# Attention with a routed mixture of experts: the last tiles in a written-out order, the first maxima ahead of the value blocks, and six rows a partition summed in SBUF

## The chip, the core and the metric

The kernel runs on one core of one Trainium2 chip. The metric is the device time of one execution in microseconds (us). The kernel before took 504.38 us, the median of 3 runs (503.53 to 505.40). One more execution was profiled; it took 505.53 us.

## The reference

The input x is (4, 256, 32, 32): B = 4 images of C = 256 channels and 1024 tokens, N = 4096 tokens in all. Cut to what matters:

```
q, k, v = 1x1 convolutions of x              # 32, 32 and 256 channels
energy  = einsum('bci,bcj->bij', q, k)       # seen as (b, h, w, h, w)
attn    = softmax(energy, axis=-1)           # over the last w alone
x = gamma * einsum('bchk,bhwkv->bcwv', v, attn) + x
t = tokens of x                              # (4, 1024, 256)
u = layer_norm(t)
t = t + u @ W1 + (memory @ u) @ W2 + bias    # memory[i, j] = i - j for 0 < i - j < 33, else 0
u = layer_norm(t)
sel = sigmoid(u @ expert_sel.T)              # 32 experts, the two best per token
t = t + sum over the two best experts e of sel_e * (relu(u @ keys_e) @ values_e)
```

## The kernel before

All arithmetic is float32, in hand-written queues: each engine has a program of its own, and semaphores (`wait_ge`, `then_inc`) tie them together. An engine works strictly in the order that is written; a step that waits holds everything behind it.

**Start.** SyncE loads the weights and the first image. TensorE makes keys and queries of image 0, then value blocks: `vT` holds 8 blocks (`KB`) of 128 positions for each of two images, block (b, j) for image b. A block is two matmuls of 128x256 into PSUM (`v_proj`, L1128) and one evacuation on DVE (`v_evac`, L803), which scales by gamma and adds `gbv`, itself scaled once on DVE (L811) when the transfers of bv, gamma and bias have landed. Block (0, j) lies in one of four half banks, every later one in `v_p`, the upper half of bank 7. TensorE makes block 0, the scores of tile 0 (`energies`, L1159, 16 quick matmuls into `X`, banks 0 to 3), blocks 1 to 4, the scores of tile 1, blocks 5 to 7.

**The 32 steps (`NT`).** The tokens are 32 tiles of 128, 8 per image. Step s starts tile s and carries on earlier ones, each stage at a lag: at lag 0 scores, maximum (DVE, L874), subtraction (DVE, L878), exponential (ScalarE, L691), sum and reciprocal (DVE, L899, L905), scaling of the probabilities (GpSimd, L510); at lag 1 `attend` (TensorE, L1234, 16 passes of 128x256), the first sum t1 (DVE, L826), squares (ScalarE, L628); at lag 2 layer-norm factors (GpSimd, L481, L483), norm (ScalarE), `turn` (TensorE transposes, L1241); at lag 3 a copy and its rest (`turned`, `turned_low`, L831), `mix` (TensorE, L1196, six matmuls of 128x512), z_hi (ScalarE), and t1b = t1 + bias (GpSimd, L496, two buffers); at lag 4 z_lo (DVE, L818), `memory` (TensorE, L1217), `second_sum` (DVE, L837), second squares, factors and norm; at lag 5 `second_turn`, `logits` (L1224), exponential, sigmoid and the two best (DVE); at lag 6 the choice as 0/1 (`chosen`, `both_chosen`) and `positions` (TensorE), which counts the tokens chosen before; at lag 7 `place`, `entry_rows`, `rows_of_slots` (DVE), which give a row number for each of the token's two copies, and `send` (GpSimd, L487): two indirect scatters of 128 rows into the DRAM tensor `slot_rows`. In each of the first 24 steps TensorE also makes a value block of the next image (`proj_work`), once the first sum of the tile before is done, since block and sum share bank 7; its evacuation stands first in DVE's next step, ahead of the maximum. From tile 2 on the scores stand at the head of TensorE's step.

**The last tiles.** After step 31, a loop on each engine goes on with the same stages in steps 32 to 36; tiles 30 and 31 go together through mix, memory and logits. Six matmuls on zeros (`DRAIN_WARM`) keep TensorE active there.

**The plan.** When the last slots are known, DVE counts tokens per expert and works out which rows make which tile of work (L961 to L998), TensorE turns the table, DVE writes it (L1008). SyncE then loads the groups of rows, each with register arithmetic per transfer; 20 groups of four tiles, the first 12 in whole tiles, the rest in halves. Per group: transposes, hidden layer, outputs; results go by indirect DMA into the DRAM tensor `out`, 8192 rows, row t for a token's first expert and row N + t for its second.

**The final sum.** When everything is sent, GpSimd issues four accumulating transfers (L595), each adds 1024 rows of the second half of `out` to the first half in DRAM, in descriptors of 8 rows (8 KB), 128 of them a transfer. SyncE waits for all four, and the kernel ends.

```
sums_d = out.rearrange("(r c n k) e -> r c n (k e)", r=2, c=SUMS, k=SUM_ROWS)
for c in range(SUMS):
    g.dma_start(sums_d[0, c], sums_d[1, c], accum_op=ALU.add, ...).then_inc(stored, 16)
```

Of the kernel before, what the change touches and what calls it, by code (L numbers as in the profile page):

```python
# [21 lines left out]
P = 128  # L22
# [18 lines left out]
NB = 4  # L41
# [3 lines left out]
SUM_ROWS = 8  # L45
BLK = 8
# [4 lines left out]
DRAIN_WARM = 6  # L51
# [12 lines left out]
def attention_moe(nc, x_cm, x_tok, wqk4, bqk4, wvT, bv, gamma, w1, w2, bias, selT, keys, values, out):  # L64
    slots_d = nc.dram_tensor("slot_rows", [NE * CAP + P, ROW], F32, kind="Internal").ap()

    with ExitStack() as ctx:
# [54 lines left out]
        t1b = sb("t1b", [P, 2, C])  # L122
# [83 lines left out]
        vv_half = vv.rearrange("p b k r n -> p (b k r) n").rearrange("p (b k) n -> p b k n", k=GROUP)  # L206
        yb = vT[:, :, :, :].rearrange("p a (b k) n -> p (a b) k n", k=GROUP)
# [18 lines left out]
        BEFORE_E, BEFORE_MAX, BEFORE_SUM, BEFORE_E1 = 1, 1, 3, 5  # L226
# [40 lines left out]
        stored = sem("stored")  # L267

# [22 lines left out]
        def row_buffer(n):  # L291

            return xin[:, n % XB] if n % XB < NB else xin_far[:, n % XB - NB]

# [57 lines left out]
        def v_no(b, j):  # L352
            return b * KB + j

# [3 lines left out]
        def _(sp):  # L358
# [56 lines left out]
            for n in range(GROUPS):  # L415
                if n == NO_PAD_GROUPS:
                    sp.wait_ge(pads_done, 16 * (PB + PR))
                load_group(n)
            sp.wait_ge(stored, 16 * SUMS)

        @block.gpsimd
        def _(pool):
# [68 lines left out]
            def add_bias(t):  # L491
# [3 lines left out]
                after(pool, t2_done, t - 1)  # L495
                g.tensor_tensor(t1b[:, t % 2], t1[:, t % 3], biasb[:, :], ALU.add).then_inc(t1b_done, 1)  # L496
# [37 lines left out]
            for s in range(NT, NT + S_POS):  # L534
                for t in tiles(s, S_TURN):
                    first_factors(t)
                if s == NT:
                    send(s - S_SEND - 1)
                if s == NT + 1:
                    rows_complete(s - S_SEND)  # L540
                    scatter_rows(s - S_SEND, 0)
                for t in tiles(s, S_NORM2):
                    second_factors(t)
                for t in tiles(s, S_MIX):
                    add_bias(t)
                if s == NT:
                    send(s - S_SEND)
                elif s == NT + 1:
                    scatter_rows(s - S_SEND, 1)
                if s > NT:  # L550
                    send(s - S_POS)
# [41 lines left out]
            sums_d = out.rearrange("(r c n k) e -> r c n (k e)", r=2, c=SUMS, k=SUM_ROWS)  # L593
            for c in range(SUMS):
                g.dma_start(sums_d[0, c], sums_d[1, c], accum_op=ALU.add,  # L595
                            max_dma_last_dim=4 * SUM_ROWS * C).then_inc(stored, 16)
        @block.scalar
        def _(act):
# [118 lines left out]
            turned(NT - S_MIX)  # L717
            columns_written(NT - S_POS)
# [692 lines left out]
```

## Time and profile before

| | |
|---|---|
| median of 3 runs | 504.38 us |
| profiled execution, its own time | 505.53 us |
| its span | 503.80 us |
| TensorE busy | 397.0 us, 79% |
| DVE / ScalarE / GpSimd busy | 335.9 / 283.6 / 297.1 us |
| start to the first attend (23.03) | 23 us |
| steps 0 to 31 | to about 277.9 us |
| last tiles and plan | to about 319.5 us |
| expert groups | to about 474 us |
| final sum and end | to 503.8 us |

TensorE's busy share is a mean over stages with different limits; a stage is read by what ends last in it. The chain of waits follows the execution back from its last instruction, at each step to what released it. The time of a run contains the span and what lies around it, 1.73 us here.

### The profile page before, as it was taken

How to read it: one execution, taken by the hardware profiler on the slowest of the kernel's cores; microseconds unless marked ns; L12 is line 12 of the kernel's file. 1: busy time of each engine (PE TensorE's matmuls, PEld its weight loads, DVE VectorE, ACT ScalarE, POOL GpSimd, SP SyncE). 2: the span in 40 equal slices, each digit the busy share in tenths (PEclk: the TensorE clock that was granted, in tenths of full speed). 3: DMA queues.
4: the chain of work that ended last, by engine and by line, in shares of the span. 5: the costliest groups of instructions: out<-in, count | busy, mean ns of one | idle time of the engine just before them, and what ended most of it. 6: DMA issues, size and time to landing. Idle time of an engine off the chain costs nothing.

```text
span 503.8 us, 10424 instructions
## 1 busy us (share of the span) xinstructions
PE 397.0 (79%) x3007; PEld 307.7 (61%) x3007; DVE 335.9 (67%) x1022; ACT 283.6 (56%) x828; POOL 297.1 (59%) x386
## 2 busy tenths in 40 slices
PE   8879999999999999999999775759686757467000
PEld 3557778777878788787778563338464546356000
DVE  1856688987879787899999536536566678478000
ACT  1144767766767676778787455248655676354000
POOL 5333546766677777678888656343566655446700
PEclk9999999999999999999999857698989879799655
DMA  6998001411111111111111111476554443331195
GB/s 208 312 213 190 25 12 37 133 45 43 55 44 54 45 43 54 34 55 54 56 65 44 43 44 54 119 247 193 167 166 130 128 138 105 107 101 45 11 208 114
DMA packets 28441, 49.58 MB, mean 98 GB/s; under 512 B 6204, under 2 KB 21966, under 8 KB 27373
## 3 DMA queue, kind: packets, MB, share of 16 engines
q1 hardware_dynamic: 20512, 26.72, 20.0%
q0 software_dynamic: 7872, 22.19, 14.3%
q8 instruction: 25, 0.41, 0.4%
q14 instruction: 32, 0.26, 0.2%
HBM read 30.77 MB, written 25.73 MB: 112 GB/s over the span
## 4 chain that ended last, share of the span: by engine, by line
PE 48%; SPq 17%; issue 13%; DVE 11%; DMA 3%; ACT 2%; POOL 2%; POOLq 0%; DVEq 0%; ACTq 0%
PE bank L1234 21%; SPq L412 8%; PE bank L1196 7%; SPq L409 5%; PE bank L1128 5%; PE bank L1217 4%; PE bank L1224 3%; DVE vT L803 2%; SPq L276 2%; PE bank L1110 2%; DVE z_lo L818 2%; DMA biasb<-bias 2%; PE bank L1208 1%; PE X L1196 1%; SPq L277 1%
## 5 line engine op out<-in xcount | busy, mean ns | idle before, releaser
L1234 PE MATMUL bank<-vT,prob 128*128 128x256 f32 x512 | 116.0, 380 | 0.7 <-DVE vT L803 0.7
L580 POOL DMA_INDIRECT out<-vT,dest x80 | 78.5, 981 | 64.3 <-DVE vT L1062 42.7
L1234 PEld LDWEIGHTS bank<-vT,prob 128*128 128x128 f32 x512 | 94.9, 190 | 13.4 <-issue 1.1
L510 POOL TENSOR_TENSOR prob<-prob,ginv 128x1024 f32<-128x1024 f32 x32 | 61.3, 1916 | 25.9 <-DVE ginv L905 25.8
L487 POOL DMA_INDIRECT slot_rows<-rows,slot x64 | 64.8, 1013 | 16.2 <-issue 16.2
L481 POOL TENSOR_TENSOR rstd<-rstd,half_neg 128x1 f32<-128x1 f32 x64 | 36.0, 562 | 57.4 <-ACT rstd L632 56.1
L747 ACT ACTIVATE prob<-X 128x512 f32<-128x512 f32 x40 | 22.3, 593 | 50.9 <-remote 19.5
L691 ACT ACTIVATE prob<-prob 128x1024 f32<-128x1024 f32 x32 | 33.9, 1059 | 22.7 <-DVE prob L878 22.7
L1062 DVE SCALAR_TENSOR_TENSOR vT<-bank,wgt,vT 128x256 f32<-128x256 f32 x80 | 33.2, 478 | 16.0 <-remote 9.5
L874 DVE TENSOR_REDUCE gmax<-X 128x32 f32<-128x1024 f32 x32 | 39.2, 1224 | 5.9 <-PE X L1159 5.8
L899 DVE TENSOR_REDUCE gsum<-prob 128x32 f32<-128x1024 f32 x32 | 38.8, 1212 | 4.4 <-ACT prob L691 4.3
L878 DVE TENSOR_TENSOR prob<-X,gmax 128x1024 f32<-128x1024 f32 x32 | 39.2, 1225 | 1.1
L1076 DVE COPY rows<-values_s 64x256 f32 x112 | 37.5, 335 | 3.2 <-issue 2.0
L1128 PE MATMUL bank<-wv,xc_or_xin 128*128 128x256 f32 x128 | 33.0, 385 | 3.9 <-DVE t L826 2.7
L803 DVE SCALAR_TENSOR_TENSOR vT<-bank,gam,gbv 128x256 f32<-128x256 f32 x32 | 15.0, 479 | 29.0 <-PE bank L1128 28.9
L628 ACT ACTIVATE squares<-t,mv 128x256 f32<-128x256 f32 x64 | 31.9, 498 | 2.6 <-DVE t L826 2.5
L769 ACT ACTIVATE k_s<-keys_s 128x128 f32 x112 | 24.6, 301 | 10.3 <-issue 10.3
L1128 PEld LDWEIGHTS bank<-wv,xc_or_xin 128*128 128x128 f32 x128 | 23.5, 189 | 10.6 <-DVE t L826 3.9
L1331 PE MATMUL X<-ident,xc_or_xin 128*128 128x128 f32 x96 | 16.0, 321 | 17.4 <-DMA xc_or_xin<-slot_rows 15.7
L1196 PE MATMUL bank<-w_hi,uT_hi 128*128 128x512 f32 x60 | 28.0, 466 | 0.0
L1343 PE MATMUL X<-prob,k_s 128*128 128x256 f32 x96 | 24.8, 404 | 2.4 <-issue 1.6
L1331 PEld LDWEIGHTS X<-ident,xc_or_xin 128*128 128x128 f32 x96 | 12.7, 165 | 22.6 <-DMA xc_or_xin<-slot_rows 17.8
(203 smaller groups left out, 907.8 us busy)
## 6 DMA issues: line engine op xcount, KB each, us to landing
xc_or_xin<-slot_rows SPq DMA_DIRECT2D x32, 130.0 KB
xt<-x_tok SPq DMA_DIRECT2D x32, 128.0 KB, 2.1
values_s<-values SPq DMA_DIRECT2D x2, 2048.0 KB, 29.5
out<-out POOLq DMA_DIRECT2D x4, 1024.0 KB, 14.6
xc_or_xin<-x_cm SPq DMA_DIRECT2D x3, 1024.0 KB, 21.8
t<-slot_rows SPq DMA_DIRECT2D x16, 130.0 KB
t<-slot_rows SPq DMA_DIRECT2D x32, 65.0 KB
xc_or_xin<-slot_rows SPq DMA_DIRECT2D x32, 65.0 KB
```

The lines of the kernel that those rows point to most:

```text
L412: sp.dma_start(row_buffer(n)[r * HALF:(r + 1) * HALF, k, :], slots_d[bass.ds(start[2 * k + r], HALF), :]).then_inc(ld_rows[n % XB], 16)
L481: g.tensor_tensor(rstd[:, t % 2, 1:2], rstd[:, t % 2, 0:1], half_neg[:, :], ALU.pow).then_inc(rstd_done, 1)
L487: g.indirect_dma_start(out=slots_d, out_offset=bass.IndirectOffsetOnAxis(ap=slot[:, t % RB, r:r + 1], axis=0), in_=rows[:, t % RB, r, :], ...
L510: g.tensor_tensor(prob[:, t % 2], prob[:, t % 2], ginv[:, t % 2].unsqueeze(2).to_broadcast([P, WT * KB, W]), ALU.mult).then_inc(prob_done, 1)
L580: g.indirect_dma_start(out=out, out_offset=bass.IndirectOffsetOnAxis(ap=dest[:, n % (2 * NB), k:k + 1], axis=0), in_=yb[:, n % NB, k, :], ...
L874: v.tensor_reduce(gmax[:, s % 2].rearrange("p (w j) -> p w j", w=WT), E.rearrange("p w (j v) -> p w j v", v=W), AX.X, ALU.max).then_inc(ma ...
L878: v.tensor_tensor(prob[:, s % 2].rearrange("p (j w) v -> p w j v", w=WT), E.rearrange("p w (j v) -> p w j v", v=W), gmax[:, s % 2].rearran ...
L899: v.tensor_reduce(gsum[:, s % 2], prob[:, s % 2], AX.X, ALU.add).then_inc(sum_done, 1)
L1076: done = v.tensor_copy(into, values_s[side, bass.ds(expert[2 * k + r], 1), :].rearrange("p e n -> p (e n)"))
L1128: mm = m.matmul(dst, x, w, start=(i == 0), stop=(i == len(terms) - 1))
L1196: mm = m.matmul(hz_at(t), u[:, t % 2, a, :], w[:, a].rearrange("p s n -> p (s n)"), start=(i == 0), stop=(i == len(terms) - 1))
L1234: mm = m.matmul(av_p, pr[:, j, :], vT[:, b % 2, j, :], start=(j == 0), stop=(j == KB - 1))
```

## The change

It has three parts.

*First tiles.* On DVE, tile 0's maximum and subtraction come first, then the scaling of gbv and three value blocks. TensorE makes tile 1's scores after block 3 instead of 4. Block (1, 0) goes to the upper half of bank 4 (`v_at`), is made once six blocks of image 0 are evacuated, and is evacuated after tile 1's subtraction; the first attend waits for the 8 blocks of image 0 and no longer for that one. Tile 2's scores come on TensorE directly after the first attend, ahead of block (1, 1); the evacuation of (1, 1) still stands ahead of tile 2's maximum.

*Last tiles.* The loops over steps 32 to 36 are replaced on the four engines by written-out lists of the same calls. attend(31) now comes first on TensorE; tiles 30 and 31 are no longer paired; the six zero matmuls are two times three. t1b has three buffers, and the bias sums of tiles 29, 30 and 31 are made by DVE (`last_bias`). GpSimd sends tile 24 before the factors of tile 30.

*Final sum.* The four transfers cover the first 3328 of 4096 rows, so each has 104 descriptors. The last 768 rows of each half are loaded into `xc_or_xin` as 128 partitions of 6 rows, the first half by SyncE, the second by ScalarE; DVE adds them in two ops of 128x768; when the four transfers are done, SyncE and ScalarE each store half of the result.

```
-BEFORE_E, BEFORE_MAX, BEFORE_SUM, BEFORE_E1 = 1, 1, 3, 5
+BEFORE_E, BEFORE_SUM, BEFORE_E1 = 1, 3, 4
+TAIL_ROWS = 6
+IN_PLACE = N - TAIL_ROWS * P
-DRAIN_WARM = 6
+DRAIN_WARM = 3
+tail = xc_or_xin[:, 0:2 * TAIL_ROWS * C].rearrange("p (r n) -> p r n", r=2)
...
+def v_at(b, j):
+    return bank[4][:, C:2 * C] if (b, j) == (1, 0) else v_p
...
 # SyncE, at its end
+for i in range(NB):
+    sp.wait_ge(y_sent[i], sent_before(GROUPS))
+sp.dma_start(tail[:, 0], tail_rows(0)).then_inc(ld_tail[0], 16)
+sp.wait_ge(tail_added, 1)
 sp.wait_ge(stored, 16 * SUMS)
+sp.dma_start(tail_rows(0)[:, tail_half(0)], tail[:, 0, tail_half(0)]).then_inc(tail_stored, 16)
+sp.wait_ge(tail_stored, 32)
...
 # GpSimd
-    after(pool, t2_done, t - 1)
-    g.tensor_tensor(t1b[:, t % 2], t1[:, t % 3], biasb[:, :], ALU.add).then_inc(t1b_done, 1)
+    after(pool, t2_done, t - 2)
+    g.tensor_tensor(t1b[:, t % 3], t1[:, t % 3], biasb[:, :], ALU.add).then_inc(t1b_done, 1)
...
-for s in range(NT, NT + S_POS):
...
+send(NT - 8)
+first_factors(NT - 2)
+send(NT - 7)
+first_row(NT - 6)
+first_factors(NT - 1)
+second_factors(NT - 4)
+second_row(NT - 6)
+second_factors(NT - 3)
+send(NT - 5)
+second_factors(NT - 2)
+send(NT - 4)
+second_factors(NT - 1)
+send(NT - 3)
...
-    g.dma_start(sums_d[0, c], sums_d[1, c], accum_op=ALU.add,
+    g.dma_start(sums_d[0][c], sums_d[1][c], accum_op=ALU.add,
...
 # ScalarE, after the step loop
+turned(NT - 3)
+columns_written(NT - 6)
+second_copy(NT - 5)
+first_norm(NT - 2)
+first_squares(NT - 1)
+second_squares(NT - 4)
+turned(NT - 2)
+second_turned(NT - 5)
+z_high(NT - 3)
+z_high(NT - 2)
+logits_exp(NT - 5)
+first_norm(NT - 1)
...
+second_norm(NT - 2)
+second_squares(NT - 1)
+second_copy(NT - 3)
+second_turned(NT - 2)
...
 # DVE, start and step loop
-dve.wait_ge(ld_bcast, 48)
-v.tensor_scalar(gbv[:, :], gbv[:, :], gam[:, 0:1], None, ALU.mult).then_inc(gbv_done, 1)
-dve.wait_ge(gbv_done, 1)
-for j in range(BEFORE_MAX):
-    v_evac(0, j)
...
-    if work:
+    if work and s > 1:
         v_evac(work[0], work[1])
...
+    if s == 1:
+        v_evac(1, 0)
...
 # DVE, after the step loop
+z_low(NT - 4)
+turned_low(NT - 3)
+place_rows(NT - 7)
+chosen(NT - 6)
+both_chosen(NT - 6)
+last_bias(NT - 3)
+last_bias(NT - 2)
+first_sum(NT - 1)
+second_sum(NT - 4)
+last_bias(NT - 1)
+place_rows(NT - 6)
...
+for r in range(2):
+    dve.wait_ge(ld_tail[r], 16)
+for i in range(2):
+    v.tensor_tensor(tail[:, 0, tail_half(i)], tail[:, 0, tail_half(i)], tail[:, 1, tail_half(i)],
+                    ALU.add).then_inc(tail_added, 1)
...
 # TensorE
-    pe.wait_ge(v_out, min(t + 1 + TB, B * KB))
+    pe.wait_ge(v_out, min(t + 1 + TB, B * KB) if t > 0 else KB)
...
+attend(NT - 1)
+memory(NT - 4)
+second_turn(NT - 5)
+turn(NT - 2)
+positions(NT - 6)
+mix(NT - 3)
+mix(NT - 2)
+logits(NT - 5)
+memory(NT - 3)
+memory(NT - 2)
+turn(NT - 1)
+second_turn(NT - 4)
+positions(NT - 5)
+logits(NT - 4)
+mix(NT - 1)
+second_turn(NT - 3)
+positions(NT - 4)
+kept_warm(DRAIN_WARM)
+memory(NT - 1)
+logits(NT - 3)
+second_turn(NT - 2)
+positions(NT - 3)
+logits(NT - 2)
+kept_warm(DRAIN_WARM)
+second_turn(NT - 1)
+positions(NT - 2)
+logits(NT - 1)
+positions(NT - 1)
```

The order of DVE's instructions at its start, before. gmax is the maximum, prob the subtraction, gbv the scaled bias, vT a value block, gsum and ginv sum and reciprocal:

```order
L811 TENSOR_SCALAR gbv<-gbv,gam 128x256
L803 SCALAR_TENSOR_TENSOR vT<-bank,gam,gbv 128x256
L874 TENSOR_REDUCE gmax<-X 128x32
L878 TENSOR_TENSOR prob<-X,gmax 128x4x8x32
L803 SCALAR_TENSOR_TENSOR vT<-bank,gam,gbv 128x256 x2
L899 TENSOR_REDUCE gsum<-prob 128x32
L905 RECIPROCAL ginv<-gsum 128x32
L803 SCALAR_TENSOR_TENSOR vT<-bank,gam,gbv 128x256 x6
L874 TENSOR_REDUCE gmax<-X 128x32
```

And now, down to the same second maximum and past it:

```order
L918 TENSOR_REDUCE gmax<-X 128x32
L922 TENSOR_TENSOR prob<-X,gmax 128x4x8x32
L927 TENSOR_SCALAR gbv<-gbv,gam 128x256
L852 SCALAR_TENSOR_TENSOR vT<-bank,gam,gbv 128x256 x3
L948 TENSOR_REDUCE gsum<-prob 128x32
L954 RECIPROCAL ginv<-gsum 128x32
L852 SCALAR_TENSOR_TENSOR vT<-bank,gam,gbv 128x256 x5
L918 TENSOR_REDUCE gmax<-X 128x32
L922 TENSOR_TENSOR prob<-X,gmax 128x4x8x32
L852 SCALAR_TENSOR_TENSOR vT<-bank,gam,gbv 128x256
```

Both the first and the second maximum have one value block fewer ahead of them, and the first also no gbv.

TensorE behind the first attend, before, then now (L1128 and L1227 are a value block, L1159 and L1258 the scores of tile 2):

```order
L1234 MATMUL bank<-vT,prob 128x256 x8
L1128 MATMUL bank<-wv,xc_or_xin 128x256 x2
L1159 MATMUL X<-k_s,q_s 32x256 x16
L1234 MATMUL bank<-vT,prob 128x256 x8
L1119 MATMUL bank<-xc_or_xin,wqk 32x256 x8
```

```order
L1333 MATMUL bank<-vT,prob 128x256 x8
L1258 MATMUL X<-k_s,q_s 32x256 x16
L1227 MATMUL bank<-wv,xc_or_xin 128x256 x2
L1333 MATMUL bank<-vT,prob 128x256 x8
L1218 MATMUL bank<-xc_or_xin,wqk 32x256 x8
```

The scores of tile 2 and block (1, 1) have changed places.

TensorE after step 31, from turn(29) (first row) on, before; the attend of tile 31 comes behind the mix that begins in the last row:

```order
L1241 MATMUL bank<-ident,u 128x128 x2
L1208 MATMUL bank<-ident,rows 128x128 x2
L1217 MATMUL bank<-z_hi,band_r 128x256
L1217 MATMUL bank<-z_lo,band_r 128x256
L1217 MATMUL bank<-z_hi,band_r 128x256
L1217 MATMUL bank<-z_lo,band_r 128x256
L1224 MATMUL bank<-sels,u2T 128x32 x2
L1180 MATMUL X<-hotb,upper 128x32
L1181 MATMUL X<-seen,ones_b 128x32
L1196 MATMUL bank<-w_hi,uT_hi 128x512
```

And now (L1340 turn, L1333 attend, L1316 memory, L1307 second_turn, L1279 and L1280 positions, L1295 mix):

```order
L1340 MATMUL bank<-ident,u 128x128 x2
L1333 MATMUL bank<-vT,prob 128x256 x8
L1316 MATMUL bank<-z_hi,band_r 128x256
L1316 MATMUL bank<-z_lo,band_r 128x256
L1316 MATMUL bank<-z_hi,band_r 128x256
L1316 MATMUL bank<-z_lo,band_r 128x256
L1307 MATMUL bank<-ident,rows 128x128 x2
L1340 MATMUL bank<-ident,u 128x128 x2
L1279 MATMUL X<-hotb,upper 128x32
L1280 MATMUL X<-seen,ones_b 128x32
L1295 MATMUL bank<-w_hi,uT_hi 128x512
```

attend(31) stands directly behind turn(29), and turn(30) ahead of the first mix.

## Rows read from the trace of the kernel before

**Rows 1.** The page's chain of waits: share of the span by engine.
```profile
PE 48%; SPq 17%; issue 13%; DVE 11%; DMA 3%; ACT 2%; POOL 2%; POOLq 0%; DVEq 0%; ACTq 0%
```

**Rows 2.** Windows: length, busy by engine (instructions), granted clock, DMA share, GB/s.
```profile
278.10:281.20 3.10, 0.12 (x2) 0.02 (x1) 1.76 (x10) 1.81 (x10) 2.47 (x4) 1.00 0.00 0
280.00:300.00 20.00, 15.36 (x59) 12.47 (x60) 9.19 (x39) 8.20 (x30) 12.01 (x17) 0.71 0.12 41
300.00:320.00 20.00, 12.16 (x57) 6.67 (x56) 13.23 (x75) 7.38 (x28) 11.52 (x15) 0.67 0.19 67
477.50:499.00 21.50, 0.00 (x0) 0.00 (x0) 0.00 (x0) 0.00 (x0) 2.24 (x3) 0.50 0.99 195
12.00:20.00 8.00, 7.22 (x75) 5.31 (x60) 6.63 (x12) 2.39 (x3) 0.99 (x1) 1.00 1.10 399
```

**Rows 3.** Chain in order of time, first tiles: start, length (us), what.
```profile
4.32 8.58 DMA biasb<-bias
...
13.80 1.14 DVE gmax L874
...
22.88 1.14 DVE gmax L874
...
28.34 1.13 PE bank L1128 x4
...
30.31 1.23 DVE gmax L874
```

**Rows 4.** Timeline, first tiles: start, length, engine, line, operation.
```profile
11.48 0.71 PE L1159 MATMUL X<-k_s,q_s 32*32 32x256 f32 x32
...
18.84 2.09 DVE L803 SCALAR_TENSOR_TENSOR vT<-bank,gam,gbv 128x256 f32<-128x256 f32 x5
```

**Rows 5.** Timeline, end of step 31; in brackets the idle time before.
```profile
277.28 1.91 POOL L510 TENSOR_TENSOR prob<-prob,ginv 128x1024 f32<-128x1024 f32 x1 [0.21 <-DVE ginv L905]
...
277.54 0.38 PE L1241 MATMUL bank<-ident,u 128*128 128x128 f32 x2
...
281.18 0.38 PE L1217 MATMUL bank<-z_hi,band_r 128*128 128x256 f32 x1 [2.98 <-DVE z_lo L818]
...
285.20 3.62 PE L1234 MATMUL bank<-vT,prob 128*128 128x256 f32 x16
```

**Rows 6.** The page's costliest groups: busy us, mean ns; idle before, releaser.
```profile
L487 POOL DMA_INDIRECT slot_rows<-rows,slot x64 | 64.8, 1013 | 16.2 <-issue 16.2
...
L628 ACT ACTIVATE squares<-t,mv 128x256 f32<-128x256 f32 x64 | 31.9, 498 | 2.6 <-DVE t L826 2.5
```

**Rows 7.** Chain in order of time, last tiles and plan.
```profile
276.24 1.48 PE bank L1196 x6
...
293.98 2.75 PE X L1196 x6
...
302.73 0.44 DVE t L837 x2
...
309.02 0.43 DVE ex L928
...
310.65 0.19 DVE hotb L848
...
311.66 0.22 DVE slot L865
...
314.41 0.10 DVE full_i L961
...
319.19 0.29 DVE u L1008
```

**Rows 8.** Tile `out` (issues, landings), and the page's DMA issues (KB, us to landing).
```profile
L595 POOL DMA_DIRECT2D out<-out x4: 992/1347/1812, 476.2 to 477.9; - x4
...
DMA to landing us min/median/max: 7.9/14.6/21.6
...
slot_rows<-pad_rows SPq DMA_DIRECT2D x1, 130.0 KB, 2.3
```

More of the change, by code:

```diff
@@ new lines, in _ @@
+            columns_written(NT - 6)
[9 more added lines that the diff above has]
+            first_norm(NT - 1)
+            second_norm(NT - 4)
+            second_squares(NT - 3)
+            turned(NT - 1)
+            second_turned(NT - 4)
+            columns_written(NT - 5)
@@ L787, in _ @@
                     transposed(n + 2)
+            for i in range(NB):
+                act.wait_ge(y_sent[i], sent_before(GROUPS))
+            a.dma_start(tail[:, 1], tail_rows(1)).then_inc(ld_tail[1], 16)
+            act.wait_ge(tail_added, 2)
+            act.wait_ge(stored, 16 * SUMS)
+            a.dma_start(tail_rows(0)[:, tail_half(1)], tail[:, 0, tail_half(1)]).then_inc(tail_stored, 16)
         @block.vector
@@ new lines, in _ @@
+            first_sum(NT - 1)
+            second_sum(NT - 4)
+            last_bias(NT - 1)
+            place_rows(NT - 6)
+            turned_low(NT - 2)
+            z_low(NT - 3)
+            z_low(NT - 2)
+            plus_one(NT - 5)
+            second_sum(NT - 3)
+            sigmoid(NT - 5)
+            two_best(NT - 5)
+            best_places(NT - 5)
+            chosen(NT - 5)
+            both_chosen(NT - 5)
+            turned_low(NT - 1)
+            place_rows(NT - 5)
+            second_sum(NT - 2)
@@ new lines, in _ @@
+            plus_one(NT - 4)
+            sigmoid(NT - 4)
+            two_best(NT - 4)
+            best_places(NT - 4)
+            chosen(NT - 4)
+            both_chosen(NT - 4)
+            z_low(NT - 1)
+            place_rows(NT - 4)
+            second_sum(NT - 1)
+            plus_one(NT - 3)
+            sigmoid(NT - 3)
+            two_best(NT - 3)
+            best_places(NT - 3)
+            chosen(NT - 3)
+            both_chosen(NT - 3)
+            place_rows(NT - 3)
+            plus_one(NT - 2)
@@ L1286, in _, with kept_warm @@
                     turn(t)
-            for s in range(NT, NT + S_POS):
-                if s >= NT + S_MIX:
-                    positions(s - S_POS)
-                for t in tiles(s, S_ROUTE):
-                    second_turn(t)
-                for t in tiles(s, S_NORM2):
-                    memory(t)
-                for t in tiles(s, S_ROUTE):
-                    logits(t)
-                if s < NT + S_MIX:
-                    positions(s - S_POS)
-                if s == NT + S_TURN:
-                    pe.wait_ge(t1_done, NT)
-                    for _ in range(DRAIN_WARM):
-                        m.matmul(bank[7], ones_b[:, :], warm[:, :], start=True, stop=True)
-                if s in (NT, NT + 1):
-                    mix(s - S_MIX)
-                for t in tiles(s, S_AV):
-                    attend(t)
-                for t in tiles(s, S_TURN):
-                    turn(t)
-                if s == NT + 1:
-                    mix(NT - 1)
+            def kept_warm(n):
+                pe.wait_ge(t1_done, NT)
+                for _ in range(n):
+                    m.matmul(bank[7], ones_b[:, :], warm[:, :], start=True, stop=True)
+            attend(NT - 1)
[26 more added lines that the diff above has]
+            positions(NT - 1)
             for _ in range(PLAN_WARM):
```

143 lines of the change are left out of this document (70 added, 73 removed).

## The prediction

> **What bounds the kernel now.** I read the chain of waits first, then its pieces in the three stretches that the change touches, then the timeline there, then the windows and the DMA landings. The chain lies on TensorE for 48% of the span and on SyncE's queue for 17% [rows 1]. The change leaves those two long stages alone (the 32 steps, and the 20 groups of expert tiles that SyncE feeds). It touches three places, each with its own limit.
>
> *The first tiles.* DVE sets the pace. Its first maximum starts at 13.80 us on the chain although the scores that it reads were ready at 12.19 (11.48 + 0.71) [rows 3, 4]: ahead of it stands the scaling of gbv, which waits for the bias transfer (4.32 + 8.58 = 12.90). The second maximum starts at 22.88, the third at 30.31, each behind a value block that TensorE could make only after an earlier step.
>
> *The last tiles.* Step 31 ends at about 277.9 us with the turn of tile 29 [rows 5]; the plan for the groups starts at 314.41 and its table is out at 319.48 [rows 7]. These 41.6 us hold little work per engine, but at each step one engine waits for another: TensorE stands 2.98 us, until 281.18, for z_lo of tile 28 [rows 5]. Its granted clock is 1.00 (2.4 GHz) in that stretch and means 0.71 and 0.67 in the next two windows, so a part of them at 1.2 GHz [rows 2]; six matmuls of a mix take 1.48 us at the one and 2.75 at the other [rows 7].
>
> *The final sum.* Nothing runs but DMA. POOL issues four accumulating transfers from 476.2 to 477.9 us and the last lands 21.6 us after its issue, at 499.5 [rows 8]. The engines are busy all along (share 0.99, 195 GB/s) [rows 2].
>
> **The change part by part. 1, first tiles.** Tile 0's maximum starts when its scores are there, at 12.3 instead of 13.72 to 13.80: 1.4 us sooner. gbv and three value blocks now lie beside the exponential, which needs about 1 us, while they need about 1.6; so the sum starts near 16.4 (the old chain: 13.80 to 17.31 is 3.5, now 4.1). Five blocks follow, 2.09 us as before [rows 4], the last of them released at about 18.35 by the fourth block's evacuation; DVE is free near 19.95. Tile 1's maximum starts there, since block (1,0) no longer stands ahead of it: 22.88 - 19.95 = 2.9 us sooner. Block (1,0) itself goes to bank 4, is made before the first attend, and is evacuated beside tile 1's exponential. Tile 1's exponential, sum, reciprocal and first sum are as long as before, so block (1,1), which stood at 28.34 [rows 3], comes at about 25.45. Tile 2's scores now precede that block on TensorE instead of following it, so 30.31 - 28.34 = 1.97 us from block to maximum become 1.6 (1.13 of matmuls and, by 2.09 for five, some 0.45 of evacuation). Tile 2's maximum starts at 27.1: **3.2 us sooner**. Afterwards nothing differs and everything shifts by that. What could take it back is the first attend: it needs tile 0's scaled probabilities, about 20.0 by the same sum. Bounds 2.0 and 3.3.
>
> **2, last tiles.** I follow the new queues with the durations of the old rows. TensorE's attend of tile 31 is first. POOL has its probabilities ready at 277.28 + 1.91 = 279.19 [rows 5]; it took 3.62 us and stood behind a mix, at 285.20. Now it ends at 282.9, 5.9 us sooner, while TensorE rests 1.3 us and not 3. memory(28), then turn(30) at 283.9: its factors on POOL stand behind both scatters of tile 24 (1.01 us each and about 0.3 between them [rows 6]), which puts u1 at 283.7, in time. mix(29) to 286.0, mix(30), 1.48, to 287.7. The longest way is then tile 31: first sum 283.4; squares 0.50 and the two small steps behind, 284.5 [rows 6]; its factors on POOL wait for the first scatter of tile 26, whose slots DVE has at 285.6, so 288.1; norm 289.1 behind logits(27); turn, copy, turned_low 291.4; mix(31) behind logits(28), 293.3; z_high, z_low 294.5; three warm matmuls and memory(31) 295.8; second_sum 296.3. Before, this sum was done at 303.17 [rows 7], so we are 6.9 us ahead. logits(29) 296.35, exponential 296.65. Then the routes: from the exponential to the chosen experts 309.02 to 310.84, 1.8 us, 0.3 for TensorE's positions and 0.7 for the slots [rows 7]. Tile 29: 298.3 for its choice. Tile 30's logits come at 299.5 (its u2 copy on ScalarE stands behind the squares of tile 31), slots 302.7; tile 31: 2.6 more, **305.3 against 314.4**. That is 9.0 us. DVE's three bias sums (each about the 0.45 of a block of that width) and POOL's freed place lie beside waits. The scatters of tile 31 begin at 305.8 and end near 308, and their landing is needed after the table, 5.1 us behind the plan's start, as before, so they stay hidden. Some 30 hand-overs are each rounded to 0.05 or nothing, and POOL or ScalarE may hold a step: I take **8 us**. The upper bound is 9.5. The lower is 5: the 6.9 already gained at second_sum(31), less 2, about what attend and three mixes gain when not at half clock.
>
> **3, the final sum.** 768 of 4096 rows leave the accumulating transfers: 3.41 MB instead of 4.19. They are loaded twice (both halves of `out`, 1.57 MB) by SyncE and ScalarE, added on DVE (two ops of 128x768, some 1.3 us, long before the rest is done) and stored, 0.79 MB, after everything else has landed. No row has an accumulate beside loads. Bounds: the accumulate moved 195 GB/s, while plain loads moved 399 GB/s from 12 to 20 us at a like share [rows 2]. Two to one is what one expects if an accumulate reads two streams and the engines' reading is the limit. Then 2 x 3.41 + 1.57 = 8.39 MB are read, exactly as before (2 x 4.19): the loads eat the whole saving. They start about 1 us before the first accumulate moves, and fill the gaps between POOL's issues: 0.5 to 1 us back. Rows also divide unevenly: a transfer has 104 descriptors of 8 KB instead of 128, and 104 is 6.5 for each of 16 engines; with seven on the busiest, 28/32 remain and not 26/32, +1.2 us. So all has landed about when it does now, 499 to 499.5. The store comes behind: a store of 130 KB takes 2.3 us from issue to landing [rows 8], the further 0.66 MB at 399 GB/s 1.6, together 3.9. **I take +3.5 us**. Lower end 0: loads wholly free and an even division, 26/32 of the 21.5 us is 4.0 saved, 3.9 back. Upper end +6.
>
> The sum is -3.2 - 8 + 3.5 = -7.7 us. The profiled execution took 505.53 us (span 503.80), 1.15 above the median of the three runs, 504.38. From the one 497.8, from the other **496.7**, which I forecast.
>
> **A rule about the division of rows.** By the rows each transfer of 128 x 8 KB took 21.5 / 4 = 5.4 us on 16 engines, eight descriptors on each [rows 2, 8]. If 104 were cut so that every used engine again had eight, that time would stay at 5.4 though a fifth less is moved, and the loads would come on top. *The Trainium skill, page "DMA: Bandwidth & Descriptors", section on why a DMA increments its semaphore by 16, says that the number of engines is the largest up to 16 that divides the slowest dimension, 13 here, which is just that case; it notes an exception for some GpSimd copies, 16 engines with the count rounded up.* No row here has a transfer whose count is not a multiple of 16. I weigh it as rival B.
>
> **The rivals.**
> A, *the loads are free* (the accumulate is held by something other than reading). The ratio 399 to 195 speaks against it; that the engines were never shown with both kinds speaks for leaving it open. End +0.5, so 504.4 - 11.2 + 0.5 = 493.7 us. Chance 0.2.
> B, *eight rows on each of 13 engines*. The busiest engine keeps its 21.5 us, plus 1.57 MB at 399 GB/s = 3.9, less 1 to 2 for the earlier start, then the store of 3.9: +6. 504.4 - 11.2 + 6 = 499.2. Chance 0.2.
> C, *the last tiles jam elsewhere*. POOL now scatters before it makes factors, and ScalarE's first_squares(31) waits for attend(31) with turned(30), second_turned(27) and z_high(29) behind it. If that costs 0.7 us in each of the seven tiles, the 8 become 3: 501.7. For it: every engine runs in order and waits of 3 us stand there now [rows 5]. Against: attend(31) is 5.9 us earlier, and that is plain. Chance 0.12.
> D, slower: *the division falls to half the engines*. 104 is 8 x 13; on eight engines a transfer takes 13/8 of 5.4 = 8.7 us, the four 35, loads and store 3.9 each, less 1: 42 against 21.5, +20. 504.4 - 11.2 + 20 = 513. It decides once the end costs more than 11.2 + 2.5 = 13.7 us. Against: nothing in the rows asks for it. Chance 0.05.
> E, *the change does not do what it says at the start*: block (1,1) still holds tile 2's maximum behind it, and if the first attend starts late the 3.2 become 1. With the rest as forecast, 498.9. Chance 0.08.
>
> **How the numbers follow.** Forecast 0.35, the rest as above. A difference under 0.5% (2.5 us: 501.9 to 506.9) is about what a measurement of this kernel can't tell from none. D is slower; half of C and a little of B's upper end fall within 0.5%; all else is faster: 0.87 faster, 0.08 same, 0.05 slower. The range: lower end from A with the upper drain bound, 504.4 - 3.3 - 9.5 + 0.5 = 492; upper end 502, which takes in B whole and half of C and leaves out D.
>
> **What the profile will show.** Right: maxima of tiles 0, 1, 2 near 12.3, 20 and 27.1 us; the step loop 3.2 us earlier; attend(31) 1.3 us after the last turn with the clock still at 1.00; 28.5 us or so from that turn to the plan's start, against 36.5; the group stage unchanged at 156.7 us; at the end loads and accumulates side by side, DMA busy about 21 us, then a store of its own, nearly 4. Wrong: a third maximum after 29; a drain over 33 us; accumulates and loads done in under 19 us (A) or over 23 (B); an end that is no longer than now.

## The result, and the profile after

The change makes the kernel faster: 491.25 us (median of 4 runs, 490.48 to 492.79) against 504.48 (4 runs, 503.53 to 505.4), a ratio of 0.9742 with the 95% interval 0.9711 to 0.9772. The forecast was 496.7, so the gain was 13.2 us and not 7.7, and the time lies 0.75 below the range. The span went from 503.8 to 489.6, 14.2 us less. Where it went is read stretch by stretch. The cuts are the third maximum of the first tiles, turn(29) on TensorE, the plan's start (`full_i` on DVE), and POOL's issue of the accumulating transfers.

| | before | after | difference | forecast |
|---|---|---|---|---|
| to turn(29) | 277.54 | 274.12 | -3.4 | -3.2 |
| turn(29) to plan | 36.8 | 26.9 | -9.9 | -8 |
| plan to accumulates | 161.9 | 162.6 | +0.8 | 0 |
| accumulates to the end | 27.6 | 25.9 | -1.7 | +3.5 |

First the timeline of the first tiles on DVE after the change (start, length, engine, line, operation; in brackets the idle time before it). It answers to [rows 3, 4].

```profile
12.26 1.23 DVE L918 TENSOR_REDUCE gmax<-X 128x32 f32<-128x1024 f32 x1 [2.10 <-PE X L1258]
...
17.73 2.09 DVE L852 SCALAR_TENSOR_TENSOR vT<-bank,gam,gbv 128x256 f32<-128x256 f32 x5
19.74 1.21 DVE L918 TENSOR_REDUCE gmax<-X 128x32 f32<-128x1024 f32 x1
...
26.45 0.48 DVE L852 SCALAR_TENSOR_TENSOR vT<-bank,gam,gbv 128x256 f32<-128x256 f32 x1 [1.22 <-PE bank L1227]
26.85 1.22 DVE L918 TENSOR_REDUCE gmax<-X 128x32 f32<-128x1024 f32 x1
```

The maxima stand at 12.26, 19.74 and 26.85 where the same view of before has 13.72, 22.80 and 30.31, each within 0.3 us of the forecast's 12.3, 20 and 27.1. The first waits only for its scores now.

Next TensorE's timeline at the end of step 31, in the same form. It answers to [rows 5].

```profile
274.12 0.38 PE L1340 MATMUL bank<-ident,u 128*128 128x128 f32 x2
275.78 3.72 PE L1333 MATMUL bank<-vT,prob 128*128 128x256 f32 x16 [1.28 <-POOL prob L531]
279.15 0.47 PE L1316 MATMUL bank<-z_hi,band_r 128*128 128x256 f32 x1
```

The idle 2.98 us for z_lo of tile 28 became 1.28 us for the probabilities of tile 31, and attend(31) starts 1.7 us behind turn(29), no longer 7.7. The windows say what this does to the clock (columns as in [rows 2]; the first four are of the change, 274.1 to 290.1, and the last is its last 3 us before the plan).

```profile
274.10:278.10 4.00, 2.72 (x14) 2.21 (x13) 2.93 (x14) 2.45 (x11) 3.53 (x3) 1.00 0.09 33
278.10:282.10 4.00, 3.91 (x23) 3.13 (x21) 1.98 (x11) 2.63 (x9) 3.00 (x5) 1.00 0.19 69
282.10:286.10 4.00, 3.62 (x23) 3.05 (x22) 2.20 (x8) 2.44 (x8) 3.47 (x6) 1.00 0.21 71
286.10:290.10 4.00, 2.96 (x18) 2.06 (x18) 3.67 (x19) 3.67 (x16) 2.70 (x5) 1.00 0.17 60
...
298.10:301.10 3.00, 1.04 (x8) 0.46 (x8) 2.13 (x12) 0.98 (x4) 1.93 (x2) 0.50 0.26 94
```

The granted clock stays at 1.00 (2.4 GHz) for these 16 us (by the clock's own records until 294.9), and all engines have work at once. Before, it was at 0.57 in the 4 us behind that idle time:

```profile
277.50:281.20 3.70, 0.72 (x6) 0.36 (x4) 2.29 (x12) 2.38 (x11) 3.07 (x4) 1.00 0.00 0
281.20:285.20 4.00, 4.00 (x16) 3.53 (x17) 2.48 (x13) 1.97 (x6) 2.61 (x5) 0.57 0.19 69
```

The chain of waits of the change in this stretch (start, length, what) leaves TensorE in its middle and runs over POOL, whose scatters and factors of the layer norms alternate there. It answers to [rows 7].

```profile
288.22 1.04 POOL slot_rows L508
289.26 0.30 issue
289.56 0.69 POOL slot_rows L508
290.26 0.29 issue
290.54 0.59 POOL rstd L502
...
301.07 0.10 DVE full_i L1055
```

Last the end: the timeline of the change from 463 us on, and what SyncE's queue waited for from 455 us on (us in total, times, longest). They answer to [rows 8].

```profile
463.06 0.34 SPq L436 DMA_DIRECT2D xc_or_xin<-out  x1
463.08 0.38 ACTq L833 DMA_DIRECT2D xc_or_xin<-out  x1
463.63 3.56 POOL L620 DMA_DIRECT2D out<-out  x4 [1.77 <-DMA out<-vT,dest]
470.81 1.83 DVE L1193 TENSOR_TENSOR xc_or_xin<-xc_or_xin 128x768 f32<-128x768 f32 x2 [16.74 <-DMA xc_or_xin<-out]
485.40 0.35 SPq L439 DMA_DIRECT2D out<-xc_or_xin  x1
485.42 0.38 ACTq L836 DMA_DIRECT2D out<-xc_or_xin  x1
```

```profile
SPq L438 <- DMA out<-out: 21.9, 1, 21.9
SPq L69 <- DMA out<-xc_or_xin: 3.0, 1, 3.0
SPq L69 <- PEq L69: 0.6, 1, 0.6
```

The stores come last, as forecast, and take 3.0 us of waiting. But behind them SyncE waits 0.6 us more, at the close of the program (L69; the view names TensorE's queue, which had been done long since; the runs below tell whose it is). That small row is the key to the term that failed.

### The profile page after: what moved, and what is told of

It is laid out like the page before. It is cut to its first block, busy times and chain, and to the rows that moved or that the text cites. A ratio compares the mean times of both kernels' runs of the same rounds, so it can differ in the third digit from the quotient of the medians.

```text
span 489.6 us, 10433 instructions
## 1 busy us (share of the span) xinstructions
PE 390.1 (80%) x3004; PEld 302.8 (62%) x3007; DVE 336.9 (69%) x1027; ACT 283.2 (58%) x828; POOL 295.4 (60%) x383
## 4 chain that ended last, share of the span: by engine, by line
PE 45%; SPq 17%; issue 15%; DVE 10%; POOL 4%; DMA 3%; ACT 2%; DVEq 0%; ACTq 0%; POOLq 0%
PE bank L1333 20%; SPq L427 9%; PE bank L1295 7%; PE bank L1227 5%; SPq L424 5%; PE bank L1316 4%; PE bank L1323 3%; PE bank L1209 2%; DVE vT L852 2%; SPq L280 2%; DVE z_lo L862 2%; DMA xc_or_xin<-out 2%; POOL slot_rows L508 1%; PE bank L1307 1%; SPq L281 1%
## 5 line engine op out<-in xcount | busy, mean ns | idle before, releaser
L1333 PE MATMUL bank<-vT,prob 128*128 128x256 f32 x512 | 116.1, 380 | 1.9 <-POOL prob L531 1.9
L1333 PEld LDWEIGHTS bank<-vT,prob 128*128 128x128 f32 x512 | 94.9, 190 | 14.4 <-POOL prob L531 2.5
L1227 PE MATMUL bank<-wv,xc_or_xin 128*128 128x256 f32 x128 | 32.6, 384 | 1.6 <-DVE t L870 1.6
L1441 PE MATMUL X<-ident,t 128*128 128x128 f32 x64 | 11.1, 325 | 25.3 <-DMA t<-slot_rows 19.2
L812 ACT ACTIVATE k_s<-keys_s 128x128 f32 x112 | 24.5, 298 | 10.1 <-issue 10.1
L1227 PEld LDWEIGHTS bank<-wv,xc_or_xin 128*128 128x128 f32 x128 | 23.6, 189 | 8.1 <-DVE t L870 2.9
L1453 PE MATMUL X<-prob,k_s 128*128 128x256 f32 x96 | 26.0, 419 | 3.1 <-issue 2.4
L1295 PE MATMUL bank<-w_hi,uT_hi 128*128 128x512 f32 x60 | 27.4, 457 | 0.1
L1441 PEld LDWEIGHTS X<-ident,t 128*128 128x128 f32 x64 | 8.6, 166 | 28.3 <-DMA t<-slot_rows 20.8
```

Source lines behind the costliest of these rows:

```text
L1227: mm = m.matmul(dst, x, w, start=(i == 0), stop=(i == len(terms) - 1))
L1295: mm = m.matmul(hz_at(t), u[:, t % 2, a, :], w[:, a].rearrange("p s n -> p (s n)"), start=(i == 0), stop=(i == len(terms) - 1))
L1333: mm = m.matmul(av_p, pr[:, j, :], vT[:, b % 2, j, :], start=(j == 0), stop=(j == KB - 1))
```

## The experiments

All have the four cuts read in their profiled execution, in us. The last column is the ratio of median times to the kernel before on the same chip; its 95% interval is 0.3 to 0.6% to either side, so the stretches of the trace tell more than it does. a_no_store, a_no_tail and a_pool_waits leave out a part of the output. The kernels from e_start to e_attend_first are made from the kernel before, those with a_ from the changed one.

| | third maximum | turn(29) to plan | plan to accumulates | to the end | time as a ratio to before |
|---|---|---|---|---|---|
| before | 30.31 | 36.8 | 161.9 | 27.61 | 1 |
| after | 26.85 | 26.9 | 162.6 | 25.93 | 0.9742 |
| e_start | 26.80 | 35.3 | 162.8 | 26.94 | 0.9940 |
| e_drain | 29.19 | 26.9 | 162.9 | 26.81 | 0.9823 |
| e_tail | 31.15 | 36.8 | 162.5 | 26.12 | 0.9984 |
| e_attend_first | 31.19 | 33.3 | 161.7 | 27.14 | 0.9962 |
| a_no_store | 26.33 | 26.9 | 162.0 | 26.01 | 0.9725 |
| a_store_x3 | 27.10 | 26.9 | 161.8 | 32.47 | 0.9890 |
| a_no_tail | 26.95 | 26.9 | 161.1 | 23.24 | 0.9694 |
| a_store_early | 27.15 | 26.8 | 162.7 | 28.29 | 0.9796 |
| a_attend_late | 27.26 | 33.3 | 127.5 | 26.17 | 0.9898 |
| a_no_warm | 27.12 | 26.7 | 127.7 | 26.10 | 0.9756 |
| a_bias_pool | 27.04 | 29.4 | 127.0 | 26.19 | 0.9786 |
| a_pool_waits | 27.10 | 26.4 | 127.2 | 30.31 | 0.9827 |
| a_e2_late | 27.56 | 26.9 | 164.8 | 26.35 | 0.9755 |
| a_two_queues | 26.99 | 26.9 | 166.8 | 26.03 | 0.9810 |

The columns tell how much executions vary: 29.2 to 31.2 for the third maximum with the old start, 26.4 to 26.9 for the same lists of the last tiles, 161.1 to 164.8 for the same group stage on all chips but one. The 127 us of that one are a matter of their own, below. No version that writes the whole output has a lower ratio than the changed kernel; the nearest are a_e2_late with 0.9755 (0.9709 to 0.9802) and a_no_warm with 0.9756 (0.9724 to 0.9788), and the intervals don't tell these three apart.

### The three parts, each alone

e_start and e_drain are the kernel before with the lines of the diff for the first tiles, or for the last, and no others; e_tail has those for the final sum. A line or two of each:

```diff
-                if s > 1:
+                if s > 2:
                     energies(s)
```
```diff
-            for s in range(NT, NT + S_POS):
+            attend(NT - 1)
+            memory(NT - 4)
...
```
```diff
+            sp.dma_start(tail[:, 0], tail_rows(0)).then_inc(ld_tail[0], 16)
```

> The kernel before with the change's part for the first tiles alone (value blocks behind the maximum and subtraction, block (1,0) in another bank, energies of tile 2 ahead of it). Theory 1, the three parts add up: turn(29) starts 3.4 us sooner (about 274.1) and the rest runs as before, span 500.4 of 503.8. Theory 2, the parts are worth more together than apart: under 2 us here. In both the group stage should still take 156.7 us; if it takes 157.5, the 0.8 us that it grew by comes with this part.

> The kernel before with the written-out lists for the last tiles alone. Theory 1, additive: from turn(29) to the plan's start 26.9 us in place of 36.9, span 9.2 to 10 us below 503.8, about 494. Theory 2: part of the 9.95 us gain of the whole change came from the earlier phases' different timing (a stall of the first tiles handed on), and less than 8 us are seen here.

> The kernel before with the change's final sum alone (last 768 rows through SBUF). Theory 1, the store lies under the end that GpSimd's queue needs behind its last accumulating DMA anyway: 1.6 us less, span about 502.2, as in the whole change. Theory 2, my prediction's term: the store is on the path, 3.5 us more, span about 507. Theory 3, the end gains only because the rows are still warm in some way that this kernel lacks: no change, 503.8.

The ratios were 0.994 (0.9904 to 0.9975), 0.9823 (0.9767 to 0.988) and 0.9984 (0.9949 to 1.0018). Their product is 0.9748; the whole change has 0.9742. So the parts add up, as far as intervals of half a per cent tell. e_start: turn(29) at 273.90, 3.6 us sooner than before. It also gained 1.5 us in last tiles that it does not touch, 35.3 against 36.8. What differs there is the clock: between turn(29) and the plan it was granted at 0.50 for 19.2 us in the kernel before and for 13.1 in e_start, while e_tail, with 19.1, took 36.8 like the kernel before. That the clock is the cause is argued from these three, not tested. Around 297 us the kernel before has 0.50 where e_start has 1.00 (windows, first before, then e_start):

```profile
297.20:301.20 4.00, 3.11 (x9) 2.43 (x9) 0.85 (x2) 1.75 (x8) 3.18 (x4) 0.50 0.18 67
```
```profile
297.50:301.50 4.00, 2.25 (x15) 0.94 (x14) 2.99 (x17) 3.22 (x12) 1.70 (x4) 1.00 0.09 33
```

e_drain: 26.9 us from turn(29) to the plan, 9.8 less, theory 1. As the whole change has 9.9 there, the 1.5 us of e_start do not come on top of the lists. The 0.8 us of the group stage belong to no part: it took 162.5 to 162.9 in all three, 161.7 in e_attend_first and 161.1 to 162.7 in four kernels with the whole change. e_tail ends 1.5 us sooner than this execution of before; the four kernels with the old final sum have 26.8 to 27.6 (mean 27.1) and the seven with the new one, undisturbed, 25.9 to 26.4 (mean 26.1), so it is worth some 1 us. That refutes the +3.5.

### Why the store costs nothing

```diff
-            sp.dma_start(tail_rows(0)[:, tail_half(0)], tail[:, 0, tail_half(0)]).then_inc(tail_stored, 16)
-            sp.wait_ge(tail_stored, 32)
```

This, with the same on ScalarE, is a_no_store. a_store_x3 repeats the stores and their wait twice more. a_pool_waits is a_no_store with one line added behind the accumulates on GpSimd:

```diff
+            pool.wait_ge(stored, 16 * SUMS)
```

> The changed kernel without the two stores of the last 768 rows (their sums are formed in SBUF and never written). Theory 1, the stores lie wholly under the end of GpSimd's queue, which outlasts the last accumulate by some 4.3 us: from POOL's issue of the accumulates to the span's end 26.0 us as with the stores (0 less). Theory 2, my prediction's term, the stores are the end of the path: 3.3 to 3.9 us less, 22.4.

> The changed kernel with the same two stores made three times, one behind the other. Theory 1 (4.3 us of cover): the first is free but for its last tenths, the second and third run past the cover, landing of the third 3 times 3.5 us behind 485.4, so 6 to 7 us more at the end (32 to 33 in place of 26.0). Theory 2 (no cover, each on the path): 7 us more too, so this run alone does not tell; read together with the run without stores, the two steps tell where the cover ends: 0 and 6 to 7, or 3.5 and 7.

> The changed kernel without the two stores (the last 768 rows' sums are not written) and with one wait more: GpSimd waits until the accumulates have landed before its program ends. Theory 1, GpSimd's end takes its 4 us from the landing on whether it waits for it or not: 26.0 us from POOL's issue, as without the wait. Theory 2, the long end is a wait of its own for the queue, which has nothing left to do once the landing is awaited by a semaphore: 22.5 to 24.

Without stores the end takes 26.01 us, with them 25.93. With three it takes 32.47, 6.5 more. So theory 1 holds: the first store is free, the next two cost 3.3 each. The last waits of SyncE say the same, of a_no_store, a_store_x3 and a_pool_waits in turn (from 455, 455 and 440 us on):

```profile
SPq L438 <- DMA out<-out: 22.0, 1, 22.0
SPq L69 <- PEq L69: 3.9, 1, 3.9
```
```profile
SPq L442 <- DMA out<-xc_or_xin: 6.0, 2, 3.0
SPq L69 <- DMA out<-xc_or_xin: 3.0, 1, 3.0
SPq L69 <- PEq L69: 0.2, 1, 0.2
```
```profile
SPq L438 <- DMA out<-out: 22.2, 1, 22.2
SPq L69 <- PEq L69: 8.1, 1, 8.1
```

Once the last accumulate has landed, the close of the program waits 3.9 us more. One store shrinks this to 0.6, three to 0.2. a_pool_waits tells whose it is. Against a_no_store it changes GpSimd alone, and the wait grows to 8.1, the end to 30.31: 4.3 us more, where theory 1 said 0 and theory 2 2 to 3.5 less. Both missed. GpSimd's closing instruction, a DRAIN, is no row of any view, but the trace holds it: in the changed kernel it runs from 464.9 to 489.3 us, 4.3 beyond the last accumulating packet; in a_pool_waits from 449.8 to 457.7, 7.9 us. It looks as if it needed about 8 us of which half can lie beside the transfers; what it does in them no run shows. From the last accumulating packet to the span's end the records give 4.54 to 4.57 us in fourteen of the sixteen kernels, the one before among them. The other two are a_pool_waits (8.7) and a_store_x3 (10.9), and in the latter the closing instruction ends at 488.9, 4.3 us behind the last accumulating packet as ever, but the third store lands at 495.0, 0.4 before the span's end. So the program ends with the later of the two.

### What the accumulates and loads share

a_no_tail takes out loads, additions and stores; the last 768 rows' sum is left out of the output. a_store_early issues the stores right behind the additions:

```diff
             sp.wait_ge(tail_added, 1)
-            sp.wait_ge(stored, 16 * SUMS)
             sp.dma_start(tail_rows(0)[:, tail_half(0)], tail[:, 0, tail_half(0)]).then_inc(tail_stored, 16)
             sp.wait_ge(tail_stored, 32)
+            sp.wait_ge(stored, 16 * SUMS)
```

> The changed kernel with its accumulates alone: the last 768 rows are neither loaded, added nor stored (left out of the output). Theory 1, the final sum is bound by the bytes read, 1.57 MB of loads among 8.39: the end is 3.7 us shorter at 415 GB/s of reads, 22.3 us from POOL's issue. Theory 2, the loads go into DMA time that the accumulates leave free: under 1 us shorter, 25 to 26.

> The changed kernel with the stores issued as soon as the additions are done (472 on), no longer behind the accumulates' landing. If DMA time is what the accumulates run out of, the 0.79 MB of stores move them 1.9 us later at the 26 GB/s of an engine, and the end with them: 27.9 us from POOL's issue. If stores of that size fit between the accumulates' reads, nothing changes, 26.0. I expect 1 to 2 more.

Without the loads the end is 2.7 us shorter (23.24), nearer to theory 1's 3.7 than to under 1: the loads cost most of what their bytes cost at the engines' reading rate. The missing 1 us is about what their head start gives: the first packet of the final sum starts 0.4 us behind POOL's issue in the changed kernel, and 1.7 in a_no_tail and in the kernel before. The early stores cost 2.4 us, somewhat more than expected of DMA time (1.9). The windows of the change show that the engines are full with both kinds, at a rate that depends on the kind:

```profile
465.00:470.00 5.00, 0.00 (x0) 0.00 (x0) 0.00 (x0) 0.00 (x0) 2.19 (x3) 0.50 1.03 345
470.00:476.00 6.00, 0.00 (x0) 0.00 (x0) 1.83 (x2) 0.00 (x0) 0.00 (x0) 0.50 1.04 214
476.00:482.00 6.00, 0.00 (x0) 0.00 (x0) 0.00 (x0) 0.00 (x0) 0.00 (x0) 0.50 1.04 213
```

345 GB/s while loads run, 213 with accumulates alone, the share 1.03 and 1.04. The packets say it more sharply: one of 6656 bytes of an accumulate took 516 ns, one of 6144 bytes of a load 234 ns (medians), 13 and 26 GB/s for an engine. So [rows 2] was read rightly, an accumulate counts twice. Added up over 16 engines, the packets of the final sum took 20.6 to 21.2 us in the four kernels with the old one and 20.8 to 21.2 in the seven with the new one; the volume is the same, and the saving of about 1 us is the earlier start of the loads. The store runs in time that the engines would spend idle.

### What the last tiles' 10 us are made of

e_attend_first is the kernel before with `attend(NT - 1)` moved ahead of the loop over the last tiles, and nothing else. The other three change one thing of the new lists:

```diff
-            attend(NT - 1)
             memory(NT - 4)
             second_turn(NT - 5)
             turn(NT - 2)
+            attend(NT - 1)
```
```diff
-            kept_warm(DRAIN_WARM)
```
```diff
 # VectorE
-            last_bias(NT - 1)
...
 # GpSimd
+            add_bias(NT - 1)
```

The first is a_attend_late. The second (at both its places) is a_no_warm. The third, for tiles 29 to 31, is a_bias_pool: in GpSimd's list the first addition stands ahead of the factors of tile 30, the others right behind the factors of tiles 30 and 31.

> The kernel before with one move alone: attend(31) ahead of all other TensorE work of the last tiles. If the late attend(31) is what the end of the last tiles waits for, most of the 10 us of the lists is seen here, 5 or more. If the chain of tiles 28 to 31 over VectorE and ScalarE in their old order sets it, under 2 us are. I take 3: attend(31) starts 5 to 8 us sooner, but its tile then waits in the old order of the other engines.

> The changed kernel with one move undone in part: attend(31) behind memory(28), second_turn(27) and turn(30) on TensorE. TensorE then stands idle for z_lo(28) again, about 3 us, attend(31) starts near 279.5 in place of 275.8 and, by theory 1 (the early attend is what keeps both the order and the clock), the plan starts 3 to 5 us later, turn(29) to plan 30 to 32 us in place of 27.0. Theory 2 (the lists' order on VectorE and ScalarE carries the gain): under 1.5 us later.

> The changed kernel without the twice 3 filling matmuls in the last tiles. The trace of the changed kernel grants 0.60 from 294 us on even with them; if they hold the clock up to there, it falls sooner and the plan starts 1 to 2 us later (28 to 29 us from turn(29)); if the real work holds it, the plan starts as before or up to 0.5 us sooner (26.5 to 27).

> The changed kernel with the three last bias additions back on GpSimd, ahead of its factors of the same tiles. There one takes 0.56 us against 0.31 on VectorE, and they stand between the prob of tile 31 and the factors of tile 30: by my prediction's reading (part of the gain is that GpSimd's queue is cleared) 0.5 to 1.5 us later; if VectorE's own queue is the one that is full, 0 to 0.5 us sooner.

The early attend alone gives 3.5 us (33.3; ratio 0.9962, 0.9926 to 0.9997). I said 3. Taken out of the new lists it costs 6.4, more than the 3 to 5 expected. The reason stands in its windows:

```profile
274.20:278.20 4.00, 1.35 (x9) 0.86 (x7) 2.83 (x13) 2.54 (x11) 3.51 (x4) 0.94 0.09 33
278.20:282.20 4.00, 2.42 (x7) 2.07 (x8) 0.10 (x1) 0.60 (x1) 2.82 (x4) 0.50 0.19 67
282.20:286.20 4.00, 3.85 (x14) 2.96 (x13) 0.15 (x1) 0.00 (x0) 0.00 (x0) 0.71 0.09 33
```
```profile
279.78 0.69 PE L1340 MATMUL bank<-ident,u 128*128 128x128 f32 x2 [3.52 <-ACT u L646]
280.26 5.10 PE L1333 MATMUL bank<-vT,prob 128*128 128x256 f32 x13
```

TensorE stands idle 3.52 us, the granted clock falls from 0.94 to 0.50, and attend(31) itself now runs at that level: its first 13 matmuls take 5.10 us (the view ends there) and all 16 take 5.75, where they took 3.72. Meanwhile DVE and ScalarE, whose lists put tile 31's sum and squares early, do almost nothing for 8 us. So order and clock come together: the same late step costs its lateness, 4.5 us (280.26 against 275.78), and 2.0 more by its own greater length, which makes the 6.4. Theory 2 is refuted.

The filling matmuls gain nothing: 26.7 without, 26.9 with. The clock does fall sooner without them, at 292.1 in place of 294.9, as the first theory said, but at no cost, in the stretch where TensorE is no longer the limit. The bias additions on GpSimd cost 2.5 us, well over the upper end expected (1.5). One part of the miss is their price: 0.56 and 0.31 us were misread, one addition of 128x256 takes 0.73 us on GpSimd and 0.42 on VectorE, so the three are 2.2 us of GpSimd. GpSimd is what the chain of the changed kernel runs over from 288 us on; it was busy 22.47 us between turn(29) and the plan there against 20.77. The granted clock was 0.62 from 290 to 294 us there, and 1.00 in the changed kernel, so the 2.5 may hold a part that is the clock's. The 9.9 us can't be split into shares by this: the early attend is worth 3.5 alone and 6.4 inside the lists, the three additions 2.5 inside them, and the order of the other steps was not tried by itself.

### The first tiles, and the group stage

```diff
-                if s == 1:
-                    energies(s + 1)
```

a_e2_late has this, and `if s > 1` again. a_two_queues lets ScalarE issue the lower halves of the slot loads of the last 8 groups:

```diff
-                        for r in range(2):
+                        for r in range(1):
...
+                    a.dma_start(row_buffer(n)[HALF:P, k, :],
+                                slots_d[bass.ds(start[2 * k + 1], HALF), :]).then_inc(ld_rows[n % XB], 16)
```

> The changed kernel with energies(2) at its old place on TensorE, behind mix and value block of step 1. If the term of the first tiles needs only maximum and subtraction ahead of the value blocks, maximum of tile 2 stays at 26.9 us and turn(29) at 274.1. If the early energies(2) carry a part, the third maximum comes 0.5 to 1.5 us later, and turn(29) with it.

> The changed kernel with the lower halves of the slot loads of the last 8 groups (32 of 112 loads) issued by ScalarE's queue, six groups ahead. SP's queue alone needs 1.2 to 1.3 us for one such load where the group stage takes 162 us, and 0.8 where it takes 127. Theory 1, the issue of the loads paces the second half of the group stage: plan to accumulates 5 to 20 us shorter where it is 162. Theory 2, buffers and the scatters pace it, and ScalarE loses what it now spends issuing: 0 to 8 us longer.

In a_e2_late the three maxima start at 12.56, 20.05 and 27.56, so the third comes 15.00 us behind the first, against 14.59 with the early energies: the move is worth 0.4 us, just below the 0.5 at which I had put a part of the gain.

a_two_queues gained nothing: the group stage took 166.8 us, where a_e2_late on the same chip took 164.8 (ratios 0.981, 0.9761 to 0.9859, and 0.9755, 0.9709 to 0.9802). Theory 1, 5 to 20 us shorter, is refuted; the time lies in the range of theory 2. The 32 half loads that stayed with SyncE took it 1.2 to 1.3 us each, no less than when it had all 64 (1.0 to 1.3 in the changed kernel). ScalarE, which issues the others ahead of its copies of the keys (L812), stood 23.5 us there in waits that the profile gives to nothing, against 2.0 in the changed kernel, and TensorE stood too:

```profile
ACT k_s L812 <- issue: 23.5, 12, 4.0
...
PEld X L1455 <- issue: 16.9, 16, 4.9
```

So halving SyncE's share does not shorten the stage. But the edit charged ScalarE with what it took from SyncE, and a gain could be hidden by that; what holds the stage is open.

## Why the prediction was wrong

The step that failed is the last term of the final sum: "The store comes behind: ... together 3.9", and with it +3.5 for the part. Its mechanism was half right. The stores do come last and do take 3.3 us to land (3.9 was my sum). But I laid them on the end of a path that I took to be the DMA's, when the rows showed the last landing at 499.5 and the span's end at 503.8 and I never asked what filled the 4.3 us between [rows 8]. It is GpSimd's close, it was there before, and the store slides under it (a_no_store: 26.01 us without it, 25.93 with it). The true end is the last accumulate plus 4.56 us, so only what moves the accumulates counts.

The second term, +1.2 us for 104 descriptors on 16 engines, was void as well. (28/32 against 26/32 of 21.5 us is 1.3 by its own figures.) In the changed kernel a transfer goes as 128 packets of 6656 bytes, with none of 8 KB among them: the 832 KB are divided evenly. The landings agree: the four transfers land 4.0 us apart, and 4.9 apart with 1024 rows each (e_start, e_drain, e_attend_first), which is 26/32; 28/32 would be 4.3. *The rule in the Trainium skill, page "DMA: Bandwidth & Descriptors", section on why a DMA increments its semaphore by 16, thus had nothing to bite on: no transfer here has a count of 104.* Rivals B and D fall with it. What stayed of the part is the volume, "the loads eat the whole saving", less the earlier start of 0.5 to 1 us. That holds, 1.0 measured over four old and seven new ends; the single pair says 1.7. Rival A (0.2) came nearest in the time, 493.7, but its mechanism is refuted: the loads are not free (a_no_tail 2.7). It came near because two errors cancelled: 4.0 us saved by free loads, and 3.9 charged for a store that costs nothing.

The last tiles: the queues followed gave 9.0 us (314.4 less 305.3 is 9.1) and 305.3 for the plan; less the first tiles' 3.2 that is 302.1, and it came at 301.07. I cut 9.0 to 8 for hand-overs; 9.9 was measured, above my upper bound of 9.5. The order was read rightly and the 1 us of caution was not needed. What the further 0.9 us is made of no run splits. The clock is the likeliest: between turn(29) and the plan it was at 0.50 for 6.1 us, where the kernel before had 19.2. The lower bound's "2, about what attend and three mixes gain when not at half clock" saw this effect, but only as something to take off. Rival C (jam in the queues, 0.12) did not appear, though a_bias_pool shows that GpSimd had little room: 2.5 us for three additions.

The first tiles: -3.2 forecast, -3.4 in the pair. The group stage's +0.8 is variation between executions. Added up, the spans missed 6.5 us (14.2 against 7.7): 5.2 in the final sum, 1.9 in the last tiles, 0.2 in the first, less the 0.8 that the group stage took, each rounded. The lower end of the range charged the store too. Without its 3.9 us the forecast would be 492.8 and the lower end 488, below the measured 491.25.

## What to carry over

Before a step is priced at the end of a program, subtract the last landing from the span's end and find the engine that fills the gap; whatever fits into it is free, and whatever moves the landing counts whole. Where TensorE idles at a hand-over between two stages, put there the longest work that is ready: in this kernel that saved its lateness and kept the clock for what followed (1.3 us idle and a clock of 1.00, against 3.5 us idle and 0.50). When steps are moved between engines, look at the engine on which the chain will run afterwards, not at the one on which it runs now.

## What the runs showed of the hardware that I had not expected

GpSimd's closing instruction took 7.9 us when nothing was in flight, and ended 4.3 us behind the last accumulating packet when begun 20 us before it. A wait for the last transfer put ahead of it made the end 4.3 us longer (a_pool_waits against a_no_store).

The same group stage took 161.1 to 164.8 us elsewhere and 127.0 to 127.7 on the chip of four kernels (a_attend_late to a_pool_waits), where the kernel before took 468.2 us. There SyncE issued 32 half loads in 25.1 us, against 41.9 in the changed kernel's profile:

```profile
347.99 25.07 SPq L427 DMA_DIRECT2D t<-slot_rows  x32
```
```profile
362.31 41.88 SPq L427 DMA_DIRECT2D t<-slot_rows  x32
```

The order on each engine is the same, and the last tiles and the end took as long as elsewhere. Between 310 and 440 us the waits that the profile gives to nothing add up to 44.1 us over the engines in the changed kernel and to 29.8 in a_no_warm on that chip. Moving loads to a second queue didn't help where the stage is long (a_two_queues), and why the chips differ stays open. For a comparison it means that the kernel before has to run on the same chip: as a ratio the changed kernel's variant a_no_warm had 0.9756 there, close to the change's 0.9742, but in microseconds 11.4 against 13.2.
